# One more expert tile inside the mixer: the step without scans takes a tile too

## The reference, cut to what matters

```
x = x + mamba(layernorm(x))      # selective scan, 1024 channels x 16 states
x = x + moe(layernorm(x))        # 8 experts, every token goes to its best 2

router_probs = softmax(x @ gate_w);  topk_w, topk_idx = top_k(router_probs, 2);  topk_w /= sum(topk_w)
h   = silu(x @ w1[e]) * (x @ w3[e])         # 512 -> 1792, for the tokens of expert e
out = sum over the two experts of topk_w * (h @ w2[e])
```

## Time and profile before

| | |
|---|---|
| time, median of 3 runs | 4637.71 us (4635.84 to 4641.01) |
| profiled execution: its time, its span | 4637.9 us, 4636.1 us |
| TensorE busy / weight loads | 4149.5 us (90%) / 3362.7 us (73%) |
| VectorE, ScalarE, GpSimd busy | 2411.8, 1932.2, 1835.0 us (52%, 42%, 40%) |
| mean granted clock of TensorE | 0.953 of full speed |
| block 2's first instruction, its first matmul | 2570.72 us, 2597.76 us |

### The profile page before, as it was taken

How to read it: one execution, slowest core, us unless ns; L and a number is a source line. 1 busy time by engine, 2 the same in 40 slices (tenths; PEclk the granted TensorE clock), 3 DMA queues, 4 the chain that set the end, 5 groups by cost and what they waited for, 6 DMA issues and landing times. The chain is left out here.

```text
span 4636.1 us, 70329 instructions
## 1 busy us (share of the span) xinstructions
PE 4149.5 (90%) x25764; PEld 3362.7 (73%) x25764; DVE 2411.8 (52%) x3197; ACT 1932.2 (42%) x4080; POOL 1835.0 (40%) x1416
## 2 busy tenths in 40 slices
PE   5777888888888888888877599999999999999999
PEld 4555667766776777667755588888888888888887
DVE  2999998998998989989987100000000000000000
ACT  5767777777777767777764000000000000000000
POOL 2767768766786687667755000000000000000000
PEclk8788999999999999999988799999999999999999
DMA  3022353545354435443533303031030303021300
GB/s 132 30 76 96 112 164 111 168 146 164 111 163 151 163 107 164 154 160 112 162 118 98 134 14 109 14 104 20 16 109 14 109 14 109 14 87 35 108 16 14
DMA packets 289343, 451.99 MB, mean 97 GB/s; under 512 B 15862, under 2 KB 183414, under 8 KB 280822
## 3 DMA queue, kind: packets, MB, share of 16 engines
q1 hardware_dynamic: 273078, 412.71, 27.1%
q0 software_dynamic: 14768, 34.41, 4.0%
q10 hardware_dynamic: 1296, 2.37, 0.1%
HBM read 920.96 MB, written 45.95 MB: 209 GB/s over the span
## 5 line engine op out<-in xcount | busy, mean ns | idle before, releaser
L546 POOL TENSOR_TENSOR hs<-hs,bc 128x1024 f32<-128x1024 f32 x512 | 1213.5, 2370 | 340.2 <-DVE hs L1114 317.7
L1114 DVE TENSOR_TENSOR_SCAN hs<-dA,pU 128x1024 f32<-128x1024 f32 x512 | 1168.8, 2283 | 53.1 <-ACT dA L651 31.2
L1562 ACT ACTIVATE gate<-pA 128x512 f32<-128x512 f32 x216 | 117.5, 544 | 1859.8 <-PE pB L1604 1859.8
L651 ACT ACTIVATE dA<-delta,aneg 128x255 f32<-128x255 f32 x2048 | 854.2, 510 | 28.5 <-DVE hs L1114 21.9
L1477 POOL DMA_INDIRECT out<-ow,trow x54 | 83.5, 1547 | 1971.5 <-DVE ow L1699 1971.5
L1604 PE MATMUL pA<-xT,w1s 128*128 128x128 f32 x6048 | 799.8, 275 | 0.7 <-ACT xT L1575 0.7
L1604 PE MATMUL pB<-xT,w3s 128*128 128x128 f32 x6048 | 799.7, 275 | 0.0
L970 PE MATMUL pY<-ident,hs 128*128 128x128 f32 x4096 | 569.0, 288 | 238.8 <-POOL hs L546 238.4
L1604 PEld LDWEIGHTS pA<-xT,w1s 128*128 128x128 f32 x6048 | 741.1, 192 | 26.4 <-issue 25.4
L970 PEld LDWEIGHTS pY<-ident,hs 128*128 128x128 f32 x4096 | 492.9, 148 | 341.4 <-issue 170.7
L1604 PEld LDWEIGHTS pB<-xT,w3s 128*128 128x128 f32 x6048 | 736.9, 192 | 0.0
(11 more groups left out here) (203 smaller groups left out, 3480.5 us busy)
## 6 DMA issues: line engine op xcount, KB each, us to landing
w1s<-in_w SPq DMA_DIRECT2D x165, 1024.0 KB
w3s<-in_w SPq DMA_DIRECT2D x165, 1024.0 KB
w2s<-in_w SPq DMA_DIRECT2D x165, 1024.0 KB
ew<-in_w SPq DMA_DIRECT2D x273, 512.0 KB, 4.3
win<-in_w_in SPq DMA_DIRECT2D x128, 512.0 KB, 3.9
bc<-bc_d SPq DMA_DIRECT2D x64, 1024.0 KB, 10.6
w1s<-in_w SPq DMA_DIRECT2D x55, 512.0 KB
w3s<-in_w SPq DMA_DIRECT2D x55, 512.0 KB
```

Source lines behind the costliest of these rows:

```text
L546: pool.tensor_tensor(hs[b][:, :, :], hs[b][:, :, :], bc[:, N + g * PN:N + (g + 1) * PN, :], ALU.mult)\
L651: e = act.activation(dA[k % NB][:, i, 1:T], delta[:, c, 1:T], ACT.Exp, scale=aneg[:, c, n:n + 1])
L1114: dve.tensor_tensor_scan(hs[b][:, :, :].rearrange("p n t -> p (n t)"), dA[b][:, :, :].rearrange("p n t -> p (n t)"), pU[:, :, :].rearrange ...
L1562: act.activation(gate[q % 2][:, 0:n, :], pA[q % 2][:, 0:n, :], ACT.Silu).then_inc(silu, 1)
```

## The change

Step 16, which has only the back part of the last group, gets a tile of an expert like steps 3 to 15. EARLY becomes 14 and so NT_SURE 50 and NT 57; `early(s)` counts step 16 in; the pick for it runs on VectorE at the end of step 15, which has no softplus beside which picks 4 to 7 stood, so they are called in an `elif`. As no step follows 16, the scaling of its result stands in ScalarE's slot 15, and its add on GpSimd after the wait for the last scatters, at the end of block 1. Block 2 finds one tile less.

```
-EARLY = STEPS - EARLY0
+EARLY = STEPS - EARLY0 + 1
...
-            return EARLY0 <= s < STEPS, EARLY0 <= s - 1 < STEPS, EARLY0 <= s + 1 < STEPS
+            return EARLY0 <= s <= STEPS, EARLY0 <= s - 1 <= STEPS, EARLY0 <= s + 1 <= STEPS
...
             each_step(pool, step)
             pool.wait_ge(scattered, 16 * 2 * TT * STEPS)
+            add_rows(EARLY - 1, STEPS - 1)
             pool.wait_ge(e_added, 16 * EARLY)
...
                     if u == 0 and early(s)[1]:
                         ge(act, ew_used, EWLOADS * jt)
                         act.activation(eow, pEx[:, :, :], ACT.Copy, scale=emeta[:, 1:2]).then_inc(e_ow, 1)
+                    if u == SLOTS - 1 and s == STEPS:
+                        ge(act, ew_used, EWLOADS * EARLY)
+                        act.activation(eow, pEx[:, :, :], ACT.Copy, scale=emeta[:, 1:2]).then_inc(e_ow, 1)
...
                     if picks:
                         pick(6)
                         pick(7)
+                elif picks:
+                    for i in range(4, E_STEPS):
+                        pick(i)
```

## The result

The changed kernel takes 4647.75 us (median of 20 runs, 4641.76 to 4651.5); the kernel before, beside it, 4637.21 us (20 runs, 4633.07 to 4641.01). The ratio is 1.0022, 95% interval 1.0015 to 1.0029: some 7 to 13 us slower, at the edge of what can be told from no change. The forecast was 4641.3 us and +3.6; the time lies in the range of 4632 to 4654.

A forecast was written before the change was run, and what follows sets the result against it. It took TensorE to bound block 2, and a chain of latencies step 16. Ranking delay 33.2, add 5.4, contention and clock 2.5, less 37.47 for the tile, gave +3.6 us: 4641.3 us, range 4632 to 4654.

The forecast's parts named there:

- Block 2's 37.47 us: In block 2, one full tile less was to save 37.47 us of TensorE time, leaving 53 tiles.
- The picks at no cost: Step 15: eight small picks, hidden while GpSimd multiplies the last scan; 0.6 us if that cover were gone.
- The rounds' price: Step 16 on TensorE: each round 3.58 us of work plus 1.22 us round trip, some 4.8 us apart.
- The contention: Weight loads beside group 14's first pair of scatters were to delay them 1.0 us, between nothing and 2 us.
- The rows' load: Step 16: the load of the tile's rows was to land in 2.7 us, at 2531.1 us; TensorE waits 3.4 us.
- The clock: Step 16: TensorE slowed after the wait for rows and after slot 10, 1.5 and 1.0 us; bounds nothing to some 4.
- The end: End of block 1: the new add, issued behind the last scatters, was to cost 5.4 us, taken whole.
- half clock all through: Rival, chance 0.09: TensorE stays at half clock in step 16, 4671 us from round 2 on, 4656 from slot 10.
- no tile less: Rival, chance 0.02: the tile taken does not lower block 2's count; +41 us, 4679 us.
- the weights come late: Rival, chance 0.08: step 16's weight loads take 6.5 us, rounds 2 to 6 1.8 us longer each; +14, 4655 us.
- TensorE never waits: Rival, chance 0.04: step 16's rows, weights and round trips cost no waits; ranking 20.9 us late, -11.2 us, 4626.5 us.
- The end is hidden: Rival, chance 0.07: the new add lies within the barrier's 6.5 us ahead of block 2; 4635.9 us.

The follow-up runs named there:

- the first profile: Profiled execution of the changed kernel against the kernel before: 4651.5 us, longest of its 20 runs; ratio of the runs 1.0022, first scatter to block 2 102.5 us.
- the second profile: The changed kernel run again with nothing altered, beside the kernel before: ratio 1.0019, first scatter of group 14 to block 2 98.8 us.
- the chain first: Changed kernel with row loads before weights, projection before the tile's turn, last group's chain before the rounds, second scatter pair after round 6's multiply: ratio 0.9981, 4624.83 us.

## Why the prediction was right, and where it was not

**Right.** Block 2's 37.47 us (37.3 found). The picks at no cost (the first scatter of group 14 follows GpSimd's work by 0.15 us in both kernels, so it didn't wait for its row numbers). The rounds' price, 4.80 us apart. That the ranking would be late by what TensorE's queue puts ahead of it. That the add lies bare at the end. That the clock never stays low through the rounds (granted 1.00 from 2544 to 2572 in the change), and that waits for weights within them are small (one piece in round 4, which was 0.6 us longer). The sign of the sum. The time lies in the stated range, but that says little: the range went from -6 to +16 us, and the change cost three times the +3.6 us of the sum. What block 2 gives back was exact; the cost in block 1 was some 15% too low.

**Mis-sized**, all in one direction, 41.1 us predicted, 49.0 found in the first profile and 45.3 in the second (about 47.8 by the medians). The terms are for the first:
- *The contention*, "I give the contention 1.0 us": 3.0 us. My upper bound of 2 us was too low.
- *The rows' load*, 2.7 us to land, from the median of the steps before: 3.7 us. With the term above the rows came 3.2 us later than predicted, counted from the first scatter.
- *The clock*, "1.5 and 1.0 us": 2.8 us at the first place (2.3 in the second profile), and at the second 2.3 in this profile, none in the second, and some 1.1 in two of the edited kernels (round 6 in 4.7 us). The bounds held.
- *The end*, 5.4 us: 6.0.
- Small ones, 1.5 us together: the second turn in slot 10, also at the low clock, and the waits for weight pieces in round 4 and in the down projection.

So the ranking was not "33 to 36 us later" but 42.9 (39.8 in the second profile), counted from the first scatter.

TensorE's wait for the rows, 3.4 us predicted, was 7.8 and 6.2 us: the first two terms, and in the first profile also the projection ahead of it that ended 1.2 us sooner after the scatter. The longer wait did not make the clock dearer: the half projection took 5.7 us behind a wait of 4.4 us as behind 7.8, and 5.2 behind 6.2. I took a middle value for each unknown cost and gave 0.77 to "within 0.2%"; the costs were links of one chain and missed together, near the upper end of +10 that I had worked out and then held for unlikely. The measured 0.22%, interval 0.15 to 0.29, lies on that border, and it came from none of the cases that I had listed for "slower".

The other cases: "half clock all through" and "no tile less" fell with the rows above; "the weights come late" fell in the change, where the rounds kept 4.8 us but for one. (Its 1.8 us a round for a landing of 6.5 us should be 6.5 - 4.8 = 1.7.) "TensorE never waits", 4626.5 us, fell by 21 us. Its floor, a tail of 53.5 + 20.9 + 5.4 = 79.8 us, was for the order as written; with the chain first the tail came to 81.5 us. "The end is hidden" fell: GpSimd's DRAIN starts only when the add has landed. In the kernel with the add between the scatters it is these that hide the add, not the barrier.

## What to carry to other kernels

This step looked half idle because it is a chain of latencies: work put in front of its links in an in-order queue delayed all that followed, though each engine had room. Put the chain's links first and let the added work fill behind, and look in each queue for what waits behind a wait: this, in all, turned the same tile from 10 us lost to 9 us gained. Loads that are wanted later should not be issued beside the transfer that everything waits for. And when the unknown costs are links of one chain, add up their upper ends too before you call a loss unlikely.

## What the runs showed of the hardware

- Two indirect scatters of 128 rows each (some 257 KB) landed 1.9 to 2.6 us after their issue ended when no weights were issued beside them, and 5.2 to 5.6 us when three loads of 512 KB were (group 14's first pair, 11 profiles).
- The load of a tile's rows, 256 KB, landed in 2.6 to 2.9 us in 13 steps of the kernel before and in 3.7 to 3.8 us in step 16 of all ten kernels that have it, where an indirect add is issued right ahead of it; the cause isn't isolated.
- GpSimd's DRAIN at the barrier took 6.36 us before the change and 6.44 in the ten profiles after, with scatters or an add ahead of it.
- After TensorE had been idle 4.4 to 7.8 us, the half projection behind took 5.2 to 5.7 us in place of 3.4, with no order by the length of the idling (4.4: 5.7; 6.1: 5.3; 6.2: 5.2; 7.8: 5.7). After the thin stretch of slot 10 round 6 was slow in the changed kernel's first profile, 5.85 us, and not in its second, 3.57, same program.
